# A Mamba-style scan with a gated low-rank feed-forward on one core: the layer-norm statistics of z from VectorE to ScalarE, and batches 1 and 2 given the division of work of batch 3

## The chip, the cores and the metric

One core of a Trainium2 chip runs the whole kernel. The metric is the device time in microseconds (us) of one execution. Three runs of the kernel before gave 533.24, 533.96 and 534.74 us, so the median is 533.96 us.

## What is computed

The inputs are x (4 batches, 512 rows, 512 channels), a context of 4 x 512 x 256, and weights. In the reference, cut to the part around the change:

```python
# hidden = ctx, z = layernorm(x)
u = silu(causal_conv4(in_proj_w @ hidden) + conv_b)
delta = softplus(dt_proj_w @ dt_lo + dt_proj_b)
state = state * exp(delta * A) + (delta * u) * B_t      # 16 states for each channel
y_t = sum over n of state[n] * C_t[n]
x = x + tanh(g_xattn) * (y + D * u) * silu(layernorm(x))
x = x + tanh(g_ffn) * ffn(layernorm(x))                 # router, top 2 of 32 groups, low rank
```

`layernorm` takes mean and variance over the last axis, with eps 1e-5. The x that stands as z is indexed so that a row of x is a channel of the scan: one 128 x 512 tile of x holds the 128 channels of one block, and its row statistics are what z of that block needs.

## The kernel before, in words

The work goes through 20 phases (`PHASE`, L46), f = 0 to 19. In batches 0 to 2 a phase is one block of 128 channels over all 512 steps: phases 0 to 3 are batch 0, 4 to 7 batch 1, 8 to 11 batch 2. Batch 3 is cut in two halves of 256 steps and takes phases 12 to 19. Below, a phase of the first three batches is called a block (block 4 is phase 4, the first of batch 1).

Within a block all engines go through 16 states, n = 0 to 15, in 8 pairs (pair p is n = 2p and 2p+1). For each state:

- ScalarE (ACT) makes the decay exp(delta * A) (`decay`, L1003, its activation L1016).
- The product dt*u*B is made in one of two ways. For the pairs in `POOL_SETS` (L24) GpSimd (POOL) multiplies du by B, broadcast over the partitions, two states in one 128x1024 instruction (`times_b`, L559, instruction L571), into one of two buffers `dbu`; the decay then goes into a PSUM bank. For the other pairs TensorE (PE) multiplies the transposed du by diagonal matrices of B (`make_dbu`, L747, L759) into a PSUM bank, and the decay goes to one of three SBUF tiles `da`. The diagonal matrices of a batch are made once: by POOL (`diagonals`, L531, L544), and for the batch's last PE pair by ACT (L986).
- VectorE (DVE) runs the scan (`scan`, L1240, L1267).
- The state is multiplied by C: by POOL in pairs (`times_c`, L574, L586), or by DVE one state at a time for the pairs in `PAIRS_BY_DVE` (L98 to L100; `times_c`, L1274, L1285). In the latter case the scan writes to PSUM and the bank is free only after the multiplication.
- PE adds the 16 products, transposed, into `p_y` (`add_y`, L774, L781).

There are three PSUM banks for these tiles (`BANKS`, `wait_for_bank`, L374), twelve state slots (`RING`), and three `da` tiles, so ACT can run only about three states ahead of DVE. Every engine has its order written out by hand in a loop over f and n: POOL L609 to L670, PE L849 to L906, ACT L1132 to L1189, DVE L1399 to L1457. All waits are on counting semaphores; an engine that waits holds all that stands behind it.

Beside the scan, block f carries: the convolution of block f+5 (`conv_first` on ACT at n = 12, L1182, then three taps on DVE at n = 10, 11, 12, L1436 to L1445; the tap at n = 10 waits for `conv_first`, L1214), softplus of block f+1, du of block f+1 on POOL (`times_u`, L549), z = silu of the normalised x (`silu_z`, L1027, with two table loads), the gate and residual of block f-1 (`gate_y` on DVE at n = 8 and 9, L1428 to L1430), and from block 5 and 6 on the feed-forward of rows finished earlier. In the turning blocks 3, 7 and 11 B and C of the next batch are stored and broadcast by SyncE (SP) (L491 to L510), and the new diagonals are made.

The statistics of z of block f+4 are taken in block f by DVE, with `bn_stats` and `bn_aggr` (`z_statistics`, L1229), at n = 1, or at n = 14 when block f is the first of a batch (L1411). Four small POOL instructions turn them into scale and bias for a whole batch (`scale_of_z`, L588), in the turning block after the C of pair 5 (L661). The x of batch b+1 that they read is loaded by SP in the first block of batch b, for b = 1 and 2 (L504 to L507):

```python
if k == 0 and b and b + 1 < B:
    eng.wait_ge(ve_x2, 2 * Q * b)
    for j in range(Q):
        load_x(b + 1, j)
```

that is in blocks 4 and 8, after `gate_y` of the block before has read the old x; in block 8 the store of row tile 2 stands ahead of it on SP (L498). The x of batches 0 and 1 is loaded in the prologue.

## Time and profile before

| | |
|---|---|
| median of three runs | 533.96 us |
| the profiled execution's own time | 533.53 us |
| its span, first to last instruction | 531.8 us |
| mean granted TensorE clock | 0.978 |
| TensorE matmul busy | 491.4 us (92%) |
| TensorE weight load busy | 368.0 us (69%) |
| VectorE busy | 462.9 us (87%) |
| ScalarE busy | 380.1 us (71%) |
| GpSimd busy | 451.9 us (85%) |

1.7 us of the own time lie around the span. The shares are means over the whole kernel; the prologue (to about 27 us) and the tail (from about 507 us) have other limits than the blocks between them. In the rows further down a window from one mark to the next is used: a mark is the moment at which DVE starts delta of the next block (L1226), at n = 7 of the present one. Marks stand at 39.16 (block 0), 66.06, 90.03, 119.06 (block 3), 146.12 (block 4), 174.64, 203.36, 234.04 (block 7), 262.77 (block 8), 292.58, 320.12, 351.49 (block 11) and 375.20 us (phase 12). A window busy to 98% on an engine has that engine as a bound; when several engines have it, a change on one of them gives nothing alone.

### The profile page before, as it was taken

The page shows a single profiled execution, that of the slowest core. Times are in us where ns is not written, and L with a number is a line of the kernel's source. Part 1 is how long each engine was busy: PE and PEld are TensorE (multiplying, and loading weights), DVE is VectorE, ACT ScalarE, POOL GpSimd, SP SyncE. Part 2 cuts the span into 40 slices and gives each one's busy share as a digit, 9 for nine tenths or more (in the row PEclk, how much of TensorE's full clock was granted, in tenths as well). Part 3 has the DMA queues.
Part 4 walks back from the last instruction along what each step waited for, and adds up shares of the span by engine and source line. Part 5 has one row for each costly group of instructions (what it writes and reads, how often), then busy time and mean ns, then how long its engine had stood idle before and what let it go on. Part 6 is the DMA issues. An engine that isn't in the chain of part 4 may idle for free.

```text
span 531.8 us, 9178 instructions
## 1 busy us (share of the span) xinstructions
PE 491.4 (92%) x3018; PEld 368.0 (69%) x3018; DVE 462.9 (87%) x846; ACT 380.1 (71%) x699; POOL 451.9 (85%) x327
## 2 busy tenths in 40 slices
PE   9989899998787999999999999999899999899688
PEld 5568788687676676668676777767566766676654
DVE  3799799799799999799999999798988989999852
ACT  4698848775876777866958776957868869768542
POOL 1389999959999999989999999889799898888910
PEclk9969799999999999999999999999999999999899
DMA  5595000126520001065230000077100000000001
GB/s 127 176 375 217 0 2 1 41 85 213 182 80 1 1 1 60 1 229 202 71 101 2 20 1 22 8 281 227 45 21 1 22 20 17 6 21 21 2 20 39
DMA packets 18704, 39.36 MB, mean 74 GB/s; under 512 B 5585, under 2 KB 6353, under 8 KB 18658
## 3 DMA queue, kind: packets, MB, share of 16 engines
q1 hardware_dynamic: 18658, 38.79, 21.4%
q8 instruction: 24, 0.39, 0.3%
q14 instruction: 22, 0.18, 0.1%
HBM read 34.33 MB, written 4.46 MB: 73 GB/s over the span
## 4 chain that ended last, share of the span: by engine, by line
PE 48%; POOL 19%; DVE 13%; ACT 10%; issue 9%; DMA 1%; DVEq 0%; SPq 0%; POOLq 0%; ACTq 0%
PE p_s L759 12%; PE p_y L781 11%; POOL state L586 9%; POOL dbu L571 7%; DVE state L1267 6%; PE p_v L814 5%; PE p_f L805 5%; PE p_tr L728 3%; PE p_v L691 2%; ACT da L1016 2%; DVE x L1216 2%; PE p_pr L703 2%; ACT pair_b L1000 1%; PE p_f L794 1%; PE p_pr L682 1%
## 5 line engine op out<-in xcount | busy, mean ns | idle before, releaser
L586 POOL TENSOR_TENSOR state<-state,c_bc 128x1024 f32<-128x1024 f32 (+1 forms) x131 | 256.7, 1970 | 21.6 <-DVE state L1267 19.2
L759 PEld LDWEIGHTS p_s<-pair_b,du_t 128*128 128x128 f32 x1072 | 140.7, 200 | 44.9 <-issue 33.4
L759 PE MATMUL p_s<-pair_b,du_t 128*128 128x128 f32 x1072 | 154.6, 287 | 16.0 <-DVE state L1267 15.8
L781 PE MATMUL p_y<-ident,state 128*128 128x128 f32 x1024 | 149.3, 276 | 0.0
L1016 ACT ACTIVATE p_s<-delta,a_neg 128x512 f32<-128x512 f32 (+1 forms) x162 | 93.7, 583 | 77.6 <-DVE state L1267 44.1
L1267 DVE TENSOR_TENSOR_SCAN state<-da,p_s 128x512 f32<-128x512 f32 (+1 forms) x116 | 134.5, 1172 | 16.0 <-PE p_s L759 13.1
L571 POOL TENSOR_TENSOR dbu<-du,pair_b 128x1024 f32<-128x1024 f32 (+1 forms) x80 | 145.3, 1819 | 0.2 <-DMA pair_b<-bc_rows 0.2
L781 PEld LDWEIGHTS p_y<-ident,state 128*128 128x128 f32 x1024 | 121.5, 144 | 23.3 <-issue 20.2
L1016 ACT ACTIVATE da<-delta,a_neg 128x512 f32<-128x512 f32 (+1 forms) x158 | 99.3, 647 | 18.5 <-DVE state L1267 18.4
L1267 DVE TENSOR_TENSOR_SCAN state<-p_s,dbu 128x512 f32<-128x512 f32 (+1 forms) x100 | 97.6, 996 | 7.6 <-POOL dbu L571 6.0
L805 PE MATMUL p_f<-u_sb,h_t 128*128 128x512 f32 x112 | 55.4, 597 | 2.4 <-DVE gw L1364 2.4
L814 PE MATMUL p_v<-v_sb,hug_t 128*128 128x512 f32 x112 | 55.4, 598 | 0.0
L1285 DVE TENSOR_TENSOR state<-p_s,c_bc 128x256 f32<-128x256 f32 (+1 forms) x58 | 30.5, 526 | 0.7
L544 POOL TENSOR_SCALAR_AFFINE_SELECT pair_b<-b_t 128x1024 f32<-128x1024 f32 x11 | 12.4, 1133 | 19.9 <-ACT b_t L972 19.9
L1267 DVE TENSOR_TENSOR_SCAN state<-p_s,carry,dbu 128x256 f32<-128x256 f32 x40 | 28.0, 734 | 0.8 <-POOL dbu L571 0.7
L805 PEld LDWEIGHTS p_f<-u_sb,h_t 128*128 128x128 f32 x112 | 18.5, 191 | 12.7 <-issue 9.6
L1267 DVE TENSOR_TENSOR_SCAN p_s<-p_s,dbu 128x512 f32<-128x512 f32 x22 | 26.8, 1217 | 0.0
L1216 DVE SCALAR_TENSOR_TENSOR u<-p_pr,cw,u 128x511 f32<-128x511 f32 (+2 forms) x33 | 24.1, 730 | 2.2 <-ACT u L936 2.1
L770 PEld LDWEIGHTS p_y<-ident,skipped 128*128 128x128 f32 x64 | 7.2, 143 | 24.5 <-issue 24.5
L814 PEld LDWEIGHTS p_v<-v_sb,hug_t 128*128 128x128 f32 x112 | 18.1, 190 | 8.4 <-issue 8.3
L556 POOL TENSOR_TENSOR du<-delta,u 128x512 f32<-128x512 f32 (+1 forms) x19 | 19.8, 1043 | 2.8 <-POOL dbu L571 2.8
L682 PE MATMUL p_pr<-cx,w_in 128*128 128x512 f32 x44 | 21.5, 612 | 0.0
(175 smaller groups left out, 640.6 us busy)
## 6 DMA issues: line engine op xcount, KB each, us to landing
c_bc<-bc_rows SPq DMA_DIRECT2D x32, 512.0 KB, 5.1
pair_b<-bc_rows SPq DMA_DIRECT2D x16, 512.0 KB, 5.5
xs<-in_x SPq DMA_DIRECT2D x16, 256.0 KB, 4.6
out<-ot SPq DMA_DIRECT2D x14, 256.0 KB, 2.0
cx<-in_ctx_t SPq DMA_DIRECT2D x4, 512.0 KB, 3.8
u_sb<-in_u_w SPq DMA_DIRECT2D x1, 1024.0 KB, 14.1
v_sb<-in_v_w SPq DMA_DIRECT2D x1, 1024.0 KB, 15.6
w_in<-in_in_w_t SPq DMA_DIRECT2D x1, 384.0 KB, 4.7
```

Source lines behind the costliest of these rows:

```text
L556: eng.tensor_tensor(du[:, 0:w], delta[:, f % 2, 0:w], u[:, (Q * b + k) % U_RING, c0:c0 + w], ALU.mult).then_inc(po_du, 1)
L571: eng.tensor_tensor(dbu[:, i % 2, :, 0:w], du[:, 0:w].unsqueeze(1).to_broadcast([P, 2, w]), rows_of_b(p)[:, :, c0:c0 + w], ALU.mult).then_ ...
L586: eng.tensor_tensor(pair, pair, c_bc[:, 2 * p:2 * p + 2, c0:c0 + w], ALU.mult).then_inc(po_cs, 1)
L682: mm = eng.matmul(conv_bank(q)[:, :], w_in[:, k, e * P:(e + 1) * P], cx[:, k, :], start=(k == 0), stop=(k == KD - 1))
L759: mm = eng.matmul(p_s[g % BANKS][:, t * P:(t + 1) * P], du_t[:, f % 2, t, :], diagonals_of(n // 2)[:, n % 2, c0 // P + t, :], start=(t == ...
L781: mm = eng.matmul(p_y[:, t, :], slot(NS * f + n)[:, t * P:(t + 1) * P], ident[:, :], is_transpose=True, start=False, stop=(n == NS - 1 and ...
L805: mm = eng.matmul(hu_bank(T)[:, :], ht_of(T)[:, k, :], u_sb[:, k, :], start=(k == 0), stop=(k == Q - 1))
L814: mm = eng.matmul(v_bank(T)[:, :], hugt_of(T)[:, k, :], v_sb[:, k, :], start=False, stop=(k == Q - 1), skip_group_check=True)
L1016: eng.activation(to, delta[:, f % 2, 0:w], ACT.Exp, scale=a_neg[:, k, n:n + 1]).then_inc(ac_da, 1)
L1216: eng.scalar_tensor_tensor(out=conv_v(q)[:, s:], in0=conv_bank(q)[:, 0:L - s], scalar=cw[:, q % Q, TAPS - 1 - s:TAPS - s], in1=conv_v(q)[: ...
L1267: eng.tensor_tensor_scan(scanned, decayed, added, first, ALU.mult, ALU.add).then_inc(ve_scan, 1)
L1285: eng.tensor_tensor(slot(g)[:, 0:w], scanned, c_bc[:, n, c0:c0 + w], ALU.mult).then_inc(ve_cs, 1)
```

## The change

Three things. (1) `z_statistics` of batches 1 to 3 goes from DVE to ACT, in three parts at n = 11, 12 and 13 of block f for block f+4, in every block f from 0 to 11: a copy with a summed output, a 128x1 activation that makes the negative mean, and a square of x minus mean with a summed output. DVE keeps only the four of batch 0. `scale_of_z` of batches 1 to 3 has three POOL instructions in place of four and moves from the turning block to the next block, between the C of pair 0 and of pair 1. (2) `POOL_SETS` of batches 1 and 2 goes from pairs 1, 3, 5, 7 to pairs 0, 2, 3, 5, 6, that of batch 3. (3) The C that DVE multiplies: before, pair 1 in blocks 3 to 11 and pair 5 in blocks 3, 7 and 11; after, pair 1 in blocks 1 and 2, and pairs 1 and 4 in blocks 4 to 11. Phases 12 to 19 are as before.

```diff
--- before.py
+++ after.py
@@ -21,7 +21,7 @@
 
 
 
-POOL_SETS = [[2, 5], [1, 3, 5, 7], [1, 3, 5, 7], [0, 2, 3, 5, 6]]
+POOL_SETS = [[2, 5]] + 3 * [[0, 2, 3, 5, 6]]
 
 
 def flamingo(nc, x, ctx_t, g_xattn, g_ffn, in_w_t, conv_w, conv_b, x_w_t, dt_w_t, dt_b, a_log, d_skip,
@@ -96,8 +96,8 @@
 
 
     PAIRS_BY_DVE = [(LAST, 7)]
-    PAIRS_BY_DVE += [(f, p) for f in range(SPLIT, F) for p in (1, 4)]
-    PAIRS_BY_DVE += [(f, 1) for f in range(Q - 1, SPLIT)] + [(f, 5) for f in range(Q - 1, SPLIT, Q)]
+    PAIRS_BY_DVE += [(f, p) for f in range(Q, F) for p in (1, 4)]
+    PAIRS_BY_DVE += [(f, 1) for f in (1, 2)]
     C_BY_DVE = [(f, n) for f in range(F) for n in range(NS) if (f, n // 2) in PAIRS_BY_DVE]
     C_BY_POOL = [(f, p) for f in range(F) for p in range(PAIRS) if (f, p) not in PAIRS_BY_DVE]
     c_by_dve = {tile: i for i, tile in enumerate(C_BY_DVE)}
@@ -202,6 +202,7 @@
         zst = sb("zst", [P, 6])
         zmv = sb("zmv", [P, Q, 2])
         zv = sb("zv", [P, 2, Q])
+        z_of = sb("z_of", [P, 3, Q])
         zr = sb("zr", [P, 2, 2, Q])
         zh = sb("zh", [P, 2, L])
         sz_t = sb("sz_t", [P, Q, P])
@@ -275,6 +276,7 @@
         ac_skip = sem("act_d_u")
         ac_pre = sem("act_residual_placed")
         ac_h = sem("act_h")
+        ac_zs = sem("act_z_statistics")
         ac_e = sem("act_exp_scores")
         ac_out = sem("act_out")
 
@@ -367,7 +369,11 @@
         def broadcasts_of_b(b, p):
             return sum(p in pool_pairs(a) for a in range(b + 1)) + (p == 0)
 
-        ZOPS = 4
+        def zops(b):
+
+
+            return 4 + 3 * b
+
         FOPS = 3
         GOPS = 9
 
@@ -586,15 +592,23 @@
                 eng.tensor_tensor(pair, pair, c_bc[:, 2 * p:2 * p + 2, c0:c0 + w], ALU.mult).then_inc(po_cs, 1)
 
             def scale_of_z(b):
-                eng.wait_ge(ve_zs, 2 * Q * (b + 1))
-                if b >= 2:
-                    eng.wait_ge(ac_z, Q * (b - 1))
+                if b:
+                    eng.wait_ge(ac_zs, 3 * Q * b)
+                    if b >= 2:
+                        eng.wait_ge(ac_z, Q * (b - 1))
+                    eng.tensor_scalar(zv[:, 0, :], z_of[:, 2, :], 1.0 / E, EPS, ALU.mult, ALU.add).then_inc(po_zs, 1)
+                    eng.wait_ge(po_zs, zops(b - 1) + 1)
+                    eng.tensor_tensor(zr[:, b % 2, 0, :], zv[:, 0, :], minus_half[:, :], ALU.pow).then_inc(po_zs, 1)
+                    eng.wait_ge(po_zs, zops(b - 1) + 2)
+                    eng.tensor_tensor(zr[:, b % 2, 1, :], z_of[:, 1, :], zr[:, b % 2, 0, :], ALU.mult).then_inc(po_zs, 1)
+                    return
+                eng.wait_ge(ve_zs, 2 * Q)
                 eng.tensor_tensor(zv[:, 0, :], zmv[:, :, 1], eps_c[:, :], ALU.add).then_inc(po_zs, 1)
-                eng.wait_ge(po_zs, ZOPS * b + 1)
+                eng.wait_ge(po_zs, 1)
                 eng.tensor_tensor(zr[:, b % 2, 0, :], zv[:, 0, :], minus_half[:, :], ALU.pow).then_inc(po_zs, 1)
-                eng.wait_ge(po_zs, ZOPS * b + 2)
+                eng.wait_ge(po_zs, 2)
                 eng.tensor_tensor(zv[:, 1, :], zmv[:, :, 0], zr[:, b % 2, 0, :], ALU.mult).then_inc(po_zs, 1)
-                eng.wait_ge(po_zs, ZOPS * b + 3)
+                eng.wait_ge(po_zs, 3)
                 eng.tensor_tensor(zr[:, b % 2, 1, :], zv[:, 1, :], minus_one[:, :], ALU.mult).then_inc(po_zs, 1)
 
             def scale_of_f(T):
@@ -629,6 +643,8 @@
                         diagonals(b, i)
                 for T in STATS.get(f - 1, [])[1:]:
                     scale_of_f(T)
+                if k == 0 and b and c0 == 0:
+                    scale_of_z(b)
                 times_c(f, 1)
                 if many and not five:
                     times_b(f, pairs[2])
@@ -658,7 +674,6 @@
                 if k and STATS.get(f):
                     scale_of_f(STATS[f][0])
                 if turning:
-                    scale_of_z(b + 1)
                     diagonals(b + 1, 1)
                 times_c(f, 6)
                 if next_first and len(pool_pairs(PHASE[f + 1][0])) == 5:
@@ -1024,9 +1039,28 @@
                 eng.activation(skipped[:, 0:w], u[:, (Q * b + k) % U_RING, c0:c0 + w], ACT.Copy,
                                scale=dsk[:, k:k + 1]).then_inc(ac_skip, 1)
 
+            def z_statistics(q, part):
+
+
+                b, k = q // Q, q % Q
+                if part == 0:
+                    eng.wait_ge(s_x[b % 2][k], 16 * (b // 2 + 1))
+                    eng.wait_ge(ve_dl, q - Q + 2)
+                    if b > 1:
+                        eng.wait_ge(po_zs, zops(b - 1))
+                    eng.activation(vsp[:, :], xs[:, b % 2, k, :], ACT.Copy,
+                                   accum_out=z_of[:, 0, k:k + 1]).then_inc(ac_zs, 1)
+                elif part == 1:
+                    eng.wait_ge(ac_zs, 3 * (q - Q) + 1)
+                    eng.activation(z_of[:, 1, k:k + 1], z_of[:, 0, k:k + 1], ACT.Copy, scale=-1.0 / E).then_inc(ac_zs, 1)
+                else:
+                    eng.wait_ge(ac_zs, 3 * (q - Q) + 2)
+                    eng.activation(vsp[:, :], xs[:, b % 2, k, :], ACT.Square, bias=z_of[:, 1, k:k + 1],
+                                   accum_out=z_of[:, 2, k:k + 1]).then_inc(ac_zs, 1)
+
             def silu_z(f):
                 b, k, c0, w = PHASE[f]
-                eng.wait_ge(po_zs, ZOPS * (b + 1))
+                eng.wait_ge(po_zs, zops(b))
                 eng.wait_ge(s_x[b % 2][k], 16 * (b // 2 + 1))
                 if f >= 2:
                     eng.wait_ge(pe_turn, TURN["sz", zh_before(f)] + 1)
@@ -1180,6 +1214,8 @@
                             copy_b(b + 1)
                     if n == 12 and f + 5 < BLOCKS:
                         conv_first(f + 5)
+                    if n in (11, 12, 13) and f + Q < BLOCKS:
+                        z_statistics(f + Q, n - 11)
                     if n == 15 and f < LAST:
                         copy_du(f + 1)
                     if f in SILU_Z and n == (0 if f == 1 or turning else 9):
@@ -1227,15 +1263,12 @@
                                          op0=ALU.max, op1=ALU.add).then_inc(ve_dl, 1)
 
             def z_statistics(q):
-                b, k = q // Q, q % Q
-                eng.wait_ge(s_x[b % 2][k], 16 * (b // 2 + 1))
+                eng.wait_ge(s_x[0][q], 16)
                 if q:
                     eng.wait_ge(ve_zs, 2 * q)
-                eng.bn_stats(zst[:, :], xs[:, b % 2, k, :]).then_inc(ve_zs, 1)
+                eng.bn_stats(zst[:, :], xs[:, 0, q, :]).then_inc(ve_zs, 1)
                 eng.wait_ge(ve_zs, 2 * q + 1)
-                if b:
-                    eng.wait_ge(po_zs, ZOPS * b)
-                eng.bn_aggr(zmv[:, k, :], zst[:, :]).then_inc(ve_zs, 1)
+                eng.bn_aggr(zmv[:, q, :], zst[:, :]).then_inc(ve_zs, 1)
 
             def scan(f, n):
                 b, k, c0, w = PHASE[f]
@@ -1408,8 +1441,6 @@
                     if f == 0 and n == 7:
                         eng.wait_ge(ve_k, 3)
                         eng.reciprocal(aw[:, :], p_y_rows[:, 2 * S:3 * S]).then_inc(ve_k, 1)
-                    if n == (1 if f % Q else 14) and f + Q < BLOCKS:
-                        z_statistics(f + Q)
                     if n == 2 and mid >= 0:
                         best_two(mid, 0)
                         best_two(mid, 1)
```

## Rows read from the trace of the kernel before

**Rows 1.** The page: busy time, share of the span and instructions of each engine

```profile
PE 491.4 (92%) x3018; PEld 368.0 (69%) x3018; DVE 462.9 (87%) x846; ACT 380.1 (71%) x699; POOL 451.9 (85%) x327
```

**Rows 2.** Windows from mark to mark: PE, PEld, DVE, ACT, POOL busy, clock

```profile
146.12:174.64 28.52, 22.60 (x159) 18.58 (x158) 28.11 (x50) 19.77 (x32) 28.16 (x17) 0.96 0.12 38
...
203.36:234.04 30.68, 30.68 (x183) 20.98 (x182) 27.22 (x46) 23.30 (x37) 29.22 (x15) 1.00 0.24 84
234.04:262.77 28.73, 28.16 (x188) 22.05 (x187) 26.97 (x43) 20.51 (x40) 28.16 (x18) 1.00 0.45 170
262.77:292.58 29.81, 27.96 (x180) 21.21 (x179) 28.86 (x51) 21.77 (x35) 29.44 (x17) 1.00 0.15 46
...
320.12:351.49 31.37, 31.37 (x189) 21.85 (x188) 27.33 (x47) 24.15 (x39) 28.15 (x15) 1.00 0.21 66
```

**Rows 3.** The chain that ended last, in order of time: start, us, what

```profile
43.45 0.67 ACT u L936
...
50.67 0.60 DVE zst L1234
...
116.72 2.36 POOL state L586
...
130.89 1.03 POOL zr L594
...
191.07 6.96 POOL state L586 x3
...
202.37 1.98 PE p_f L805 x4
204.35 0.89 PE p_s L759 x8
```

**Rows 4.** Groups by form: instructions, shapes, count, busy us, mean ns, idle before

```profile
L571 POOL TENSOR_TENSOR dbu<-du,pair_b 128x1024 f32<-128x1024 f32 x40 | 94.4, 2366 | 0.2 <-DMA pair_b<-bc_rows 0.2
L1285 DVE TENSOR_TENSOR state<-p_s,c_bc 128x512 f32<-128x512 f32 x24 | 16.4, 684 | 0.4
L544 POOL TENSOR_SCALAR_AFFINE_SELECT pair_b<-b_t 128x1024 f32<-128x1024 f32 x11 | 12.4, 1133 | 19.9 <-ACT b_t L972 19.9
L1033 ACT ACTIVATE zh<-xs,zr 128x512 f32<-128x512 f32 x12 | 9.7, 813 | 0.1
L963 ACT ACTIVATE vsp<-vsp 128x512 f32<-128x512 f32 x12 | 7.5, 621 | 0.0
L1088 ACT ACTIVATION_READ_ACCUMULATOR p_f<-p_f,nmx 128x1 f32 x14 | 2.7, 191 | 0.0
L1038 ACT ACT_TABLE_LOAD x15 | 19.2, 1283 | 0.3
```

**Rows 5.** Timeline of block 4, n = 9 to 11: DVE, SP and ACT

```profile
149.54 0.67 DVE L1301 TENSOR_TENSOR x<-p_y,xs 128x512 f32<-128x512 f32 x1
...
150.23 1.77 SPq L410 DMA_DIRECT2D xs<-in_x  x4
...
150.67 0.76 ACT L936 ACTIVATE u<-p_pr,cb,cw 128x512 f32<-128x512 f32 x1
...
151.84 0.73 DVE L1216 SCALAR_TENSOR_TENSOR u<-p_pr,cw,u 128x511 f32<-128x511 f32 x1
...
152.57 1.19 DVE L1267 TENSOR_TENSOR_SCAN state<-p_s,dbu 128x512 f32<-128x512 f32 x1
```

**Rows 6.** The loads of x issued at 150.23 and at 267.82, to landing

```profile
DMA to landing us min/median/max: 4.9/4.9/4.9
...
DMA to landing us min/median/max: 4.1/4.1/4.1
```

**Rows 7.** Timeline of blocks 4 and 8: POOL's C of pair 5, SP's load, DVE's tap

```profile
157.69 2.36 POOL L586 TENSOR_TENSOR state<-state,c_bc 128x1024 f32<-128x1024 f32 x1
...
267.82 3.41 SPq L410 DMA_DIRECT2D xs<-in_x  x4
...
269.34 0.75 DVE L1216 SCALAR_TENSOR_TENSOR u<-p_pr,cw,u 128x511 f32<-128x511 f32 x1 [0.44 <-ACT u L936]
```

## The prediction

> **What bounds the kernel now.** The page's shares come first [rows 1]: PE 92%, DVE 87%, POOL 85%, ACT 71%. Three engines are close together, so a mean says little; the windows from mark to mark say more [rows 2]. In block 4 to 5 (146.12 to 174.64) DVE is busy 28.11 and POOL 28.16 of 28.52 us, PE only 22.60. The windows up to 320.12 that are not at a turn of PE's load (from the marks of blocks 5, 7, 8 and 9) look alike: POOL at 98 to 99%, DVE at 94 to 99%. Only the two windows before and into a turn, 203.36 to 234.04 and 320.12 to 351.49, have PE at 100% and POOL with 1.5 and 3.2 us to spare. Last, the chain in order of time [rows 3] names the owner of each stretch: ACT in block 0 up to 46 us (its `conv_first` stands on it), then DVE with the statistics of z on it, PE to 116, POOL alone from 116.72 to 200 (rows of C products, 2.32 us apiece: 6.96 for three), and PE from 202 on, with ACT and DVE between its stretches in block 8. The reader is to see that time can be won only where all engines of a window have room.
>
> **The price of each part.** POOL's pair instruction is 2.36 us, 2.32 apart [rows 3, 4]. A C product on DVE is 0.68, some 0.6 of it as a step in the queue [rows 4]. A PE tile of `make_dbu` is 0.89 [rows 3]. The statistics on DVE are 0.60 on the chain [rows 3] and about 0.1 more for the aggregation: 0.7. A POOL diagonal is 1.1 [rows 4].
>
> On ACT the trace has no copy or square with a summed output. The copy lies between 0.62 (immediate operands) and 0.81 (two pointers), the square likewise with one pointer; each is followed by a read of the accumulator, 0.19 [rows 4]. The 128x1 step costs at least about 0.1 in the queue and at most the 0.19 of that read. I take 0.75 + 0.15 + 0.85 = 1.75 us a block (bounds 1.4 and 2.2). ACT has 7 to 9 us idle in each of the windows shown [rows 2], so its busy time alone moves nothing there. What counts is where it stands in the queue: the first pass is at n = 11, ahead of `conv_first` at n = 12, for which DVE's first tap at n = 10 waits.
>
> Work of an ordinary block of batches 1 and 2 (4, 5, 6, 8, 9, 10): POOL 5 products with B and 6 with C against 4 and 7, so nothing. DVE two C more (1.2), statistics less (0.7): +0.5. PE two tiles fewer: -1.8. In turning blocks 7 and 11 POOL has one more pair instruction (+2.3), and DVE the same C and no statistics: -0.7. Block 3: C of pairs 1 and 5 goes back to POOL. Blocks 1 and 2: pair 1 goes to DVE, POOL -2.3 and DVE +0.5 each, with PE on the chain: nothing. Over the kernel POOL has 8 products with B more and 6 with C fewer, two diagonals fewer (-2.2, at turns 3 and 7), and three short `scale_of_z` of three instructions, whose long one stays (1.03 [rows 3]): -0.3 each. SP issues two broadcasts of B more; all B it needs early is issued early, and PE's diagonals no longer use the pairs that POOL took, so I cost it at nothing; the cover is the six or more states before those pairs are scanned.
>
> **The sum, mark by mark, as a lag against before.**
> (a) Blocks 0 to 2. ACT's first pass stands on the chain in block 0 ahead of `conv_first` [rows 3]: +0.75. Two statistics leave DVE's part of the chain: -1.4. Lag -0.7.
> (b) Block 3. DVE saves two C and one statistics at n = 1 to 3 (1.9), so POOL's C of pair 2 comes at about 115.0 instead of 116.72. From there to the product of pair 3 in block 4, at which DVE waits today, POOL has today ten pair instructions, du, three diagonals and the scale of z (27.1 us, ending at 143.8); after, eleven, du and two diagonals (28.8, ending at 143.8). So nothing is won: lag -0.7 at mark 4.
> (c) The new wait in block 4. The x that the first pass reads at n = 11 is the x of batch 2. Its load goes out at 150.23, right behind `gate_y` (149.54 + 0.67), and lands after 4.9 [rows 5, 6]. Today nobody needs it before n = 14. After the change ACT, which is at n = 12 at 150.67, stands until it lands; `conv_first` stands behind it, and DVE's tap behind that. With C of n = 8 putting `gate_y` back by 0.6: landing 155.7, first pass 0.75, decay 0.62, `conv_first` 0.7, so the tap can start at 157.8. Without the wait it would start at 151.84 + 1.2 = 153.1. DVE stands 4.7 us. The scan of n = 11, which ends at 153.8 today, ends at 159.6. POOL today starts C of pair 5 at 157.69 [rows 7], 3.9 us after that scan; this distance absorbs part. From its own work POOL could start at 156.7, and stands 2.9 us. DVE has 0.4 idle in that window [rows 2] and regains nothing; POOL is full through blocks 4 to 6. By the scan of n = 6 in block 6, POOL's count gives +4.2 and DVE's +4.5 (it regains the 1.5 us that it waits there for POOL today); less the 0.7 of (a), the lag is +3.7.
> (d) Window 203 to 234. PE sets it at 30.68; after, 28.9, with POOL 29.2 of work but able to start earlier. -1.8: lag +1.9.
> (e) Window 234 to 262. PE 1.8 less, POOL +1.0 (a pair more, a diagonal less), ACT in a solid row: I take -0.9, lag +1.0.
> (f) The new wait in block 8. The load goes out at 267.82, behind the store, and lands after 4.1 [rows 6, 7]. The same addition: 0.4 later, landing 272.3, tap possible at 274.5 against 270.1 with the extra C (today 269.34, with 0.44 of waiting for ACT in it). Scan n = 11 is 0.8 + 4.3 later. POOL had run early, so the whole counts: lag +6.1.
> (g) Blocks 9 and 10 to 320: DVE and POOL full, small idle parts against +0.5 of C: lag +5.7. Window 320 to 351, PE-bound: -1.8, then a little into the turn, -0.4. Lag +3.5. Batch 3 and the tail are as before and keep it.
> 533.53 + 3.5 = 537.0 us. The profiled execution is 0.4 below the median of the runs, so against that it is +3.0. About 0.3% (1.6 us) is what a measurement of this kernel can tell from no change.
>
> **A rule weighed.** In the rows PE holds the chain in two long stretches and is 100% busy in two windows, though its weight loads are busy 21 to 22 of some 31 us there [rows 2]. The Trainium skill, page "Perfetto Trace Analysis", section "Identifying the Most-Contended Engine", says that matmul busy time is no good measure of TensorE's distance from its limit, and that weight-load busy time is a better one. By that, TensorE with 69% is the least loaded of the four and taking work from it gives nothing.
>
> **Rivals.**
> Rival 1, faster: the waits are absorbed. Place: blocks 4 and 8, between the tap at n = 10 and C of pair 5. Price: 4.7 and 4.3 us on DVE. For it: POOL is 3.9 us behind in block 4, and PE has 6 us idle in that window [rows 2, 7]. Against it: DVE is full, and in block 8 the tap already waits for ACT. It decides where x lands before ACT asks or the lag regained exceeds 6 us. Without both waits my steps leave -0.7, then -1.8, -0.4 and -1.9 partly limited by POOL: -3.0, 530.5 us. Chance 0.13.
> Rival 2, no difference: half of the waits is absorbed, 533.5 + 0.3 = 533.8 us. Chance 0.15.
> Rival 3, slower still: PE with less work gives nothing, because POOL and DVE have the same windows; (d), and the first part of the last step of (g), drop out: 537.0 + 1.8 + 1.8 = 540.6 us. For it: POOL 29.2 of 30.7 in the window of (d). Against it: 3.2 us of room before block 11. It decides when POOL's count reaches the pair products later than PE would. This is also where the page's rule of the last paragraph leads. Chance 0.20.
> Rival 4: ACT must load another table for each square. From the rows a load is 1.28, two for each of 12 blocks 31 us, of which ACT's idle time would hide half: about 550 us. In this kernel copy and absolute value run between exponentials with no load among them: the 15 loads of L1038 are those of the 15 silu groups [rows 4]. Chance 0.02. The Trainium skill, page "ScalarE: Activation LUTs", section "Table sets: the hidden batching unit", has cheap functions in every set, naming relu, copy, identity and abs; square is not in that sentence, and no row here shows it.
> My forecast: 0.50.
>
> **The numbers.** The likeliest case gives 537.0; its own range is 535 to 539, from the bounds of ACT's parts and of the landing. The 8 in 10 reach to 541 for rival 3, and down to 533 with most of rival 2. Rival 1, a small part of rival 2 and rival 4 are left out. Faster by over 0.3% is rival 1, 0.13; within it rival 2, 0.15; slower the forecast, rival 3 and rival 4, 0.72.
>
> **What would show it.** In the changed kernel DVE's taps should wait for ACT's `conv_first` for 4 to 5 us in blocks 4 and 8, and ACT for the load of xs just before; elsewhere the tap should wait under 1 us. Windows of blocks 4 and 8 should be 4 to 6 us longer, those of blocks 6 and 10 about 1.8 shorter with PE no longer at 100%. In batch 0 no window should differ by over 1 us. ACT's table loads at L1038's place should stay at 15. I am wrong if ACT does not stand before the landing, or if POOL is still at 98% in blocks 5 to 7 after the wait and the mark of block 7 has no lag.

## The result, and the profile after

The changed kernel takes 543.2 us (median of four runs, 542.46 to 543.5) against 533.6 us for the kernel before in the same job (532.96 to 534.74). The ratio is 1.0175, 95% interval 1.0154 to 1.0197. It is slower by 9.6 us between the medians (9.3 by the ratio), where the prediction had 3.0 against the median, 3.5 against the profiled execution, and a range to 541. The profiled execution took 543.2 us, its span 541.4. Times and ratios below are of runs at the usual granted clock; only product_later has others (580.92 and 597.97 us, at a mean clock of 0.932 and 0.822), and its trace is of the first of these.

The engines' totals on the page after, which answer to [rows 1]:

```profile
PE 485.9 (90%) x2890; PEld 357.7 (66%) x2890; DVE 460.9 (85%) x834; ACT 398.2 (74%) x759; POOL 454.4 (84%) x324
## 4 chain that ended last, share of the span: by engine, by line
PE 35%; POOL 28%; DVE 14%; issue 11%; ACT 8%; DMA 2%; DVEq 0%; SPq 0%; POOLq 0%; ACTq 0%
```

PE lost 5.5 us of work, DVE 2.0, POOL gained 2.5 and ACT 18, and every share but ACT's fell. On the chain that ended last PE fell from 48% to 35% and POOL rose from 19% to 28%. Work that merely moved cannot explain a longer time in which three engines are less busy; waiting can.

The windows between the same marks as before show where the time came in (after: 67.04, 120.07 and so on; same columns as [rows 2]):

```profile
38.87:67.04 28.17, 23.98 (x167) 21.45 (x168) 22.16 (x23) 23.24 (x43) 23.46 (x11) 0.88 0.30 111
...
120.07:148.41 28.34, 21.99 (x156) 18.86 (x154) 23.43 (x25) 20.49 (x40) 28.09 (x17) 0.94 0.61 215
148.41:181.54 33.13, 24.01 (x137) 18.72 (x136) 27.89 (x49) 21.58 (x38) 29.84 (x17) 0.81 0.11 33
181.54:212.29 30.75, 28.34 (x165) 20.94 (x164) 27.59 (x47) 22.66 (x39) 28.46 (x16) 0.93 0.00 1
212.29:242.03 29.74, 29.36 (x170) 19.56 (x169) 27.69 (x46) 24.91 (x42) 28.02 (x15) 1.00 0.21 75
...
271.40:303.00 31.60, 26.67 (x164) 19.36 (x163) 28.48 (x49) 22.66 (x40) 29.14 (x17) 1.00 0.14 43
303.00:332.10 29.10, 26.17 (x164) 19.37 (x163) 27.51 (x46) 23.66 (x41) 28.49 (x16) 1.00 0.03 10
```

Against the marks of before, the lag is +1.0 at mark 1, +2.3 at mark 4, +6.9 at 5, +8.9 at 6, +8.0 at 7, +8.6 at 8, +10.4 at 9, +12.0 at 10, +10.4 at 11 and +9.1 at 13, and stays there. The windows of blocks 4 and 8 hold the forecast waits (33.13 against 28.52, 31.60 against 29.81). But the windows from marks 5 and 9 hold no load of x and are 2.0 and 1.6 us longer all the same. In the last row above DVE has 1.6 us idle, POOL 0.6, PE 2.9. In the window before and into turn 7, PE's relief is there: 29.74 instead of 30.68, and PE, busy 29.36 us of it, is still the fullest engine.

Block 4 after, in the timeline, around the wait:

```profile
153.02 0.68 DVE L1318 TENSOR_TENSOR state<-p_s,c_bc 128x512 f32<-128x512 f32 x1
...
157.30 0.63 ACT L1051 ACTIVATE vsp<-xs 128x512 f32<-128x512 f32 x1 [5.19 <-DMA xs<-in_x]
158.54 0.76 ACT L951 ACTIVATE u<-p_pr,cb,cw 128x512 f32<-128x512 f32 x1
...
159.33 0.75 DVE L1252 SCALAR_TENSOR_TENSOR u<-p_pr,cw,u 128x511 f32<-128x511 f32 x1 [3.92 <-ACT u L951]
```

ACT stands 5.19 us for x; `conv_first` is behind it; the tap stands 3.92. In block 8 the same two waits are 3.3 and 2.4. The step that was forecast happened, somewhat smaller on DVE (3.9 and 2.4 for 4.7 and 4.3).

What was not forecast as a wait is in the sums of waits between 120 and 370 us (who <- for whom: us in all, times, longest):

```profile
DVE state L1300 <- POOL dbu L577: 10.2, 7, 4.3
ACT vsp L1051 <- DMA xs<-in_x: 8.4, 2, 5.2
DVE u L1252 <- ACT u L951: 6.6, 3, 3.9
POOL state L592 <- DVE state L1300: 5.9, 7, 2.0
```

DVE waits for POOL seven times, nearly always at n = 6, and POOL waits for DVE seven times. In the kernel before, between 120 and 360 us, DVE waited for the same tile twice:

```profile
DVE state L1267 <- POOL dbu L571: 4.1, 2, 2.7
```

Two engines that wait for each other in turn make a loop. One turn of it, POOL in block 5 and 6 and the scan that waits:

```profile
192.11 2.37 POOL L592 TENSOR_TENSOR state<-state,c_bc 128x1024 f32<-128x1024 f32 x1 [2.02 <-DVE state L1300]
194.44 2.37 POOL L577 TENSOR_TENSOR dbu<-du,pair_b 128x1024 f32<-128x1024 f32 x1
...
206.91 2.37 POOL L577 TENSOR_TENSOR dbu<-du,pair_b 128x1024 f32<-128x1024 f32 x1
209.31 1.22 DVE L1300 TENSOR_TENSOR_SCAN state<-p_s,dbu 128x512 f32<-128x512 f32 x1 [1.42 <-POOL dbu L577]
...
221.21 2.36 POOL L592 TENSOR_TENSOR state<-state,c_bc 128x1024 f32<-128x1024 f32 x1 [1.20 <-DVE state L1300]
```

From C of pair 5 (192.11, released by the scan of n = 11) POOL makes seven pair instructions and one `scale_of_f` until the product of pair 3 is there (209.3, 17.2 us); DVE goes from the scan of n = 6 to that of n = 11 with two C of pair 4 and its other work (11.9 us); then POOL starts C of pair 5 again (221.21). 29.1 us for a turn, and the window from mark 9 is 29.10. Before the change there was one pair instruction fewer in the first part and no C in the second; by the same rows that is about 25.6 us (an estimate: 29.1 less 2.3 and twice 0.6), shorter than any of these windows, so the loop did not bind.

The window from mark 5 is 30.75, though, and the loop is only 29.2 of it. The rest is a wait of DVE for PE at n = 9, between the scans of n = 6 and n = 11:

```profile
186.07 1.23 DVE L1300 TENSOR_TENSOR_SCAN p_s<-da,p_s 128x512 f32<-128x512 f32 x1 [1.56 <-PE p_s L774]
```

Three of the runs below have the same loop in this block and a shorter wait there: 0.63, 1.17 and 1.24 us with windows of 29.81, 30.35 and 30.41 (batch0_c2, behind_conv2, other_x). Window less wait is 29.2 each time. The wait falls behind a stretch of PE at the lower clock (see the last section). So in block 5 the loop made about 0.5 us of the 2.0, and in block 9, where the clock was at its full level throughout, all 1.6.

### The profile page after: what moved, and what is told of

Its sections match the earlier page's. It is cut to its first block, busy times and chain, and to the rows that moved or that the text cites. A ratio compares the mean times of both kernels' runs of the same rounds, so it can differ in the third digit from the quotient of the medians.

```text
span 541.4 us, 8962 instructions
## 1 busy us (share of the span) xinstructions
PE 485.9 (90%) x2890; PEld 357.7 (66%) x2890; DVE 460.9 (85%) x834; ACT 398.2 (74%) x759; POOL 454.4 (84%) x324
## 4 chain that ended last, share of the span: by engine, by line
PE 35%; POOL 28%; DVE 14%; issue 11%; ACT 8%; DMA 2%; DVEq 0%; SPq 0%; POOLq 0%; ACTq 0%
POOL state L592 15%; POOL dbu L577 11%; PE p_y L796 8%; PE p_s L774 8%; DVE state L1300 5%; PE p_v L829 4%; PE p_f L820 3%; DVE p_s L1300 3%; PE p_tr L743 3%; PE p_v L706 2%; ACT da L1031 2%; DVE x L1252 2%; ACT p_s L1031 1%; DMA xs<-in_x 1%; DVE x L1334 1%
## 5 line engine op out<-in xcount | busy, mean ns | idle before, releaser
L592 POOL TENSOR_TENSOR state<-state,c_bc 128x1024 f32<-128x1024 f32 (+1 forms) x125 | 243.4, 1955 | 26.2 <-DVE state L1300 24.0
L577 POOL TENSOR_TENSOR dbu<-du,pair_b 128x1024 f32<-128x1024 f32 (+1 forms) x88 | 164.8, 1872 | 0.2 <-DMA pair_b<-bc_rows 0.2
L774 PE MATMUL p_s<-pair_b,du_t 128*128 128x128 f32 x944 | 139.4, 290 | 25.4 <-DVE state L1300 17.3
L774 PEld LDWEIGHTS p_s<-pair_b,du_t 128*128 128x128 f32 x944 | 125.7, 202 | 49.6 <-issue 41.0
L1300 DVE TENSOR_TENSOR_SCAN state<-p_s,dbu 128x512 f32<-128x512 f32 (+1 forms) x138 | 143.4, 1055 | 17.6 <-POOL dbu L577 12.8
L1031 ACT ACTIVATE da<-delta,a_neg 128x512 f32<-128x512 f32 (+1 forms) x142 | 87.9, 640 | 12.8 <-DVE state L1300 12.7
L1300 DVE TENSOR_TENSOR_SCAN state<-da,p_s 128x512 f32<-128x512 f32 (+1 forms) x66 | 74.2, 1144 | 8.9 <-PE p_s L774 7.1
L1300 DVE TENSOR_TENSOR_SCAN p_s<-da,p_s 128x512 f32<-128x512 f32 (+1 forms) x52 | 54.8, 1054 | 3.4 <-PE p_s L774 3.2
L1318 DVE TENSOR_TENSOR state<-p_s,c_bc 128x512 f32<-128x512 f32 (+1 forms) x70 | 38.7, 553 | 0.7
L785 PEld LDWEIGHTS p_y<-ident,skipped 128*128 128x128 f32 x64 | 7.3, 147 | 27.1 <-issue 27.1
L987 ACT ACTIVATE sz_t<-p_tr,gx 128x512 f32<-128x512 f32 (+1 forms) x20 | 12.0, 602 | 14.9 <-PE p_tr L743 14.6
```

What stands on the lines that cost most here:

```text
L577: eng.tensor_tensor(dbu[:, i % 2, :, 0:w], du[:, 0:w].unsqueeze(1).to_broadcast([P, 2, w]), rows_of_b(p)[:, :, c0:c0 + w], ALU.mult).then_ ...
L592: eng.tensor_tensor(pair, pair, c_bc[:, 2 * p:2 * p + 2, c0:c0 + w], ALU.mult).then_inc(po_cs, 1)
L774: mm = eng.matmul(p_s[g % BANKS][:, t * P:(t + 1) * P], du_t[:, f % 2, t, :], diagonals_of(n // 2)[:, n % 2, c0 // P + t, :], start=(t == ...
L1031: eng.activation(to, delta[:, f % 2, 0:w], ACT.Exp, scale=a_neg[:, k, n:n + 1]).then_inc(ac_da, 1)
L1300: eng.tensor_tensor_scan(scanned, decayed, added, first, ALU.mult, ALU.add).then_inc(ve_scan, 1)
L1318: eng.tensor_tensor(slot(g)[:, 0:w], scanned, c_bc[:, n, c0:c0 + w], ALU.mult).then_inc(ve_cs, 1)
```

## The experiments

The three suspects are the wait for x, this loop, and batch 0. Twelve kernels were run. Ratios are to the kernel before in the same job.

**The two halves of the change.** Statistics alone: the changed file with the old division of work. The other half alone: the old file with the new one.

```diff
-POOL_SETS = [[2, 5]] + 3 * [[0, 2, 3, 5, 6]]
+POOL_SETS = [[2, 5], [1, 3, 5, 7], [1, 3, 5, 7], [0, 2, 3, 5, 6]]
```

(and the old `PAIRS_BY_DVE`; the other half is the reverse edit on the kernel before.)

> The statistics of z on ScalarE as in the change, with POOL_SETS and the division of the C products as before. Theory A (the waits for x in blocks 4 and 8 are most of the loss): ScalarE stands 3 to 5 us for the load in each of them, DVE's first tap stands behind it, and a good part reaches the end: 537 to 540 us. Theory B (a loop between GpSimd and VectorE in the five-pair order is most of the loss): the loop is not there, POOL is 3.9 us behind and absorbs the waits: 533 to 535.5 us.

Measured: 538.89 us, ratio 1.0094 (1.0062 to 1.0126).

> POOL_SETS and the division of the C products as in the change, the statistics of z on DVE as before. Theory A: no new wait for x, so about as before, 532.5 to 535 us. Theory B: the loop is there (pair 3's product stands seven pair instructions behind C of pair 5, and DVE has two more C products in it), the windows of blocks 5 and 9 stay 1.5 to 2 us longer than before and none of the batch 1 and 2 windows has an engine at 98%: 537 to 541 us.

Measured: 545.68 us, ratio 1.0204 (1.0167 to 1.0241), 4.7 us above what theory B allowed.

Neither half is free, and the new sets without the statistics are worse than the whole change. Theory A fails as the only cause (sets alone, with no wait for x at all, lose 11.5 us), and so does theory B: with the loop away the statistics still cost 4.7. In statistics alone mark 8 comes 1.0 us earlier than before, and then the window from mark 8 is 33.75 against 29.81 us. The waits there, between 262 and 297 us:

```profile
DVE u L1252 <- ACT u L951: 5.5, 1, 5.5
PEld p_s L774 <- ACT du_t L987: 5.4, 1, 5.4
PE p_s L774 <- DVE state L1300: 5.2, 1, 5.2
ACT vsp L1051 <- DMA xs<-in_x: 4.4, 1, 4.4
```

One wait of 5.5 us on DVE lengthened the window by 3.9; most of it was not absorbed, in a window in which DVE had 0.95 us and POOL 0.37 us idle before. In block 4 of the same run ACT stood 1.1 us for x and DVE 1.9 behind it, and that was absorbed: the window is 30.19 us, and 30.22 in stats_late below, which has no such wait.

**The wait for x taken away.** The changed kernel, reading other data at the two places:

```diff
+                here = (b - 1) % 2 if k == 0 and b > 1 else b % 2
                 if part == 0:
-                    eng.wait_ge(s_x[b % 2][k], 16 * (b // 2 + 1))
+                    if here == b % 2:
+                        eng.wait_ge(s_x[b % 2][k], 16 * (b // 2 + 1))
...
-                    eng.activation(vsp[:, :], xs[:, b % 2, k, :], ACT.Copy,
+                    eng.activation(vsp[:, :], xs[:, here, k, :], ACT.Copy,
```

> The changed kernel, but the statistics of the first block of batches 2 and 3 are taken from the x of the batch before (already loaded), so that ScalarE does the same work without waiting for a load; this part of z is scaled by the wrong statistics. Theory A: DVE's wait of 3.9 and 2.4 us at the tap goes and 5 to 7 us with it: 536 to 538 us. Theory B: the windows of blocks 4 and 8 get shorter by 2 us each at most, because the loop then sets their length too: 539 to 541.5 us.

Measured: 538.91 us, ratio 1.0094 (1.0061 to 1.0126). 4.3 us come back, between the two expectations. In the traces it is 3.0 in the window of block 4 (30.16 for 33.13) and 1.7 in that of block 8 (29.94 for 31.60), where DVE's waits had been 3.9 and 2.4: about a quarter of them had been absorbed. The loop remains:

```profile
DVE state L1302 <- POOL dbu L577: 10.5, 6, 4.3
POOL state L592 <- DVE state L1302: 6.1, 7, 1.7
```

**The same wait, with `conv_first` ahead of it.** The changed kernel:

```diff
-                    if n in (11, 12, 13) and f + Q < BLOCKS:
-                        z_statistics(f + Q, n - 11)
+                    if n in (12, 13, 14) and f + Q < BLOCKS:
+                        z_statistics(f + Q, n - 12)
```

> The changed kernel with ScalarE's statistics at n = 12, 13, 14, behind conv_first instead of ahead of it. ScalarE still stands for x in blocks 4 and 8. If the loss goes through DVE's tap that waits for conv_first: 3 to 4 us of the 4.3 come back, 539 to 540.5 us, and the tap waits under 1 us. If it goes through the decays behind the wait: 542 to 543.5 us.

Measured: 538.61 us, ratio 1.0093 (1.0062 to 1.0124), a little below the expected range. As much comes back as in other_x, but not all for the same reason: in the trace mark 1 already comes 0.65 us earlier than after the change, since in block 0, too, ACT's first pass now stands behind `conv_first`. The windows of blocks 4 and 8 give 2.9 and 1.7. The waits between 120 and 370 us:

```profile
ACT vsp L1051 <- DMA xs<-in_x: 0.9, 2, 0.6
DVE u L1252 <- ACT u L951: 0.3, 1, 0.3
```

One reserve: ACT itself stood only 0.9 us, since it asks later and since the load landed 2.3 us after its issue in block 4, not 4.1 to 4.4 as in the changed kernel. So this run fits the place ahead of `conv_first` as the fault, but some of it is a quicker load, and it does not separate the tap from the decays that also stood behind the wait.

**The loop shortened.** The changed kernel, in the blocks of batches 1 and 2:

```diff
+                early = five and w == L
+                if early:
+                    times_b(f, pairs[2])
                 times_c(f, 0)
-                if five:
+                if five and not early:
                     times_b(f, pairs[2])
-                elif many or len(pairs) == 3:
+                elif not early and many or len(pairs) == 3:
                     times_b(f, pairs[1])
```

> The changed kernel, but in the blocks of batches 1 and 2 POOL makes the product of pair 3 with B before C of pair 0 of the same block, one pair instruction (2.3 us) earlier in the loop. Theory A: the waits for x are untouched, 542.5 to 544 us. Theory B: the loop is shorter by up to 2.3 us a block in the blocks where it binds (5, 6, 8, 9, 10), DVE's wait for dbu at n = 6 (1.1 to 1.4 us in each) goes: 537 to 540.5 us.

Measured: 535.03 us (ten runs, 533.95 to 540.74), ratio 1.0032 (1.0002 to 1.0063). 8.2 us come back from exchanging two instructions whose work is the same, more than expected. Block 5's window and block 9's, the ones without any load, are now

```profile
177.31:205.69 28.38, 26.93 (x164) 19.76 (x163) 27.56 (x47) 22.28 (x39) 28.11 (x15) 0.95 0.00 1
295.33:322.94 27.61, 25.77 (x163) 19.25 (x162) 27.44 (x46) 22.73 (x40) 27.34 (x15) 1.00 0.03 10
```

instead of 30.75 and 29.10 us, with DVE or POOL at 99% again, and DVE's wait for dbu, in the same stretch, is 3.4 us in three places instead of 10.2 in seven. The windows to marks 4 and 5 gained 2.3 and 2.5, the second in part because ACT stood only 1.8 us for x there and not 5.2; those of blocks 5, 7 and 9 gained 2.4, 1.1 and 1.5. Of block 5's 2.4 us, 0.9 is DVE's shorter wait for PE at n = 9 (0.65 us).

**The loop lengthened**, by having the same product after C of pair 2:

```diff
-                if five:
+                if five and w < L:
                     times_b(f, pairs[2])
...
                 times_c(f, 2)
+                if five and w == L:
+                    times_b(f, pairs[2])
```

> The changed kernel with POOL's product of pair 3 one pair instruction later than in the change, after C of pair 2 instead of after C of pair 0 (C of pair 1 is DVE's), in the eight blocks of batches 1 and 2. The loop theory: 2.3 us for each of the blocks in which it binds, seven or eight: 557 to 562 us. If the gain of the earlier product came from something else (the scans' order against the banks): 543 to 548 us.

Measured: 570.69 and 575.58 us, ratio 1.073 (1.0687 to 1.0773); the median of all four runs is 578.25. The direction is right and the size above the expected range: 30 us more than the change, 3.7 a block. In the trace, whose own time is 580.92, DVE waits for POOL eight times, 34.6 us in all; the chain shows why it is two instructions' time and not one:

```profile
213.31 1.14 DVE state L1302
214.52 2.37 POOL state L592
216.89 2.31 POOL dbu L577
219.22 1.22 DVE state L1302
```

C of pair 2 must wait for the scan of n = 5, so the product comes two pair instructions (4.7 us) behind that scan, and the scan of n = 6 stands 4.2 us for it.

**The loop on the sets alone.** The same edit for the early product, on the kernel with the new sets and DVE's statistics.

> POOL_SETS and the C products as in the change, statistics on DVE, and POOL's product of pair 3 before C of pair 0. The loop theory: the same gain as on the changed kernel, 8 us, from 545.7 to 536 to 539 us; what is left above 534 is DVE's own work in the loop. If the gain on the changed kernel was from an interplay with ScalarE's statistics: 542 to 546 us.

Measured: 539.9 us, ratio 1.011 (1.0083 to 1.0136). 5.8 us come back, less than 8, and the time is 0.9 above the expected range. What remains above before, 5.6 us, is more than the changed kernel with the same edit has (535.03). In that kernel DVE has nothing of the statistics of batches 1 to 3: with two more C in a block on DVE, taking them off it is worth some 5 us, between runs of two jobs.

**Another place for DVE's C.**

```diff
-    PAIRS_BY_DVE += [(f, p) for f in range(Q, F) for p in (1, 4)]
+    PAIRS_BY_DVE += [(f, p) for f in range(SPLIT, F) for p in (1, 4)]
+    PAIRS_BY_DVE += [(f, p) for f in range(Q, SPLIT) for p in (1, 7)]
```

> The changed kernel with C of pair 7 instead of pair 4 by DVE in batches 1 and 2. Each engine has the same work; only the place changes. The loop theory: POOL has one pair instruction fewer between C of pair 5 and the product of pair 3 (2.3 us), and DVE 1.2 us less between the scans of n = 6 and n = 11, so it falls as with the earlier product: 534 to 539 us. If only the amount of work on each engine counts: 542.5 to 544 us.

Measured: 548.35 us, ratio 1.0254 (1.0228 to 1.028). Both expectations miss; it is slower than the change. The loop at n = 6 did go (two waits of DVE for dbu between 120 and 370 us instead of seven), but others came, here between 150 and 370 us:

```profile
POOL state L593 <- DVE state L1301: 14.0, 8, 3.3
ACT sz_t L988 <- PE p_tr L744: 13.4, 7, 3.2
...
PEld p_s L775 <- ACT h_t L988: 13.0, 5, 3.3
...
PE p_s L775 <- DVE state L1319: 11.9, 5, 3.1
```

With C of pairs 7 and 1 on DVE, at n = 14, 15, 2 and 3, PE waits for DVE to free banks just where it has the block's transposes and scores, and the chain from 180 to 247 us lies mostly on PE. I read it so; no run took that apart.

**Batch 0.** The changed kernel with batch 0's C as before the change:

```diff
-    PAIRS_BY_DVE += [(f, 1) for f in (1, 2)]
+    PAIRS_BY_DVE += [(Q - 1, 1), (Q - 1, 5)]
```

> The changed kernel, but in batch 0 DVE multiplies the same C as before the change (pairs 1 and 5 of block 3, none in blocks 1 and 2). If DVE's C of pair 1 in block 1 is what made the first window 1.3 us longer, and POOL's two more pair instructions in block 3 what made the window to mark 4 longer, mark 4 comes 3 to 5 us earlier and the time is 539 to 541 us. If the loop of batch 1 fills whatever is gained before it: 542.5 to 544 us.

Measured: 537.83 us, ratio 1.0071 (1.0043 to 1.0098). 5.4 us come back. Mark 4 was expected 3 to 5 us earlier and comes 3.7 earlier than in the changed kernel (1.4 earlier than before the change); the time is below the expected range. The window to mark 1 is 25.94 instead of 28.17, that to mark 4 26.51 instead of 28.34. Of the 2.2 us in the first, 1.5 are the two C products that stood on the chain there: from ACT's decays to PE's next `p_s` the chain takes 5.9 us after the change and 4.4 with this edit. The other 0.7 is that piece of PE itself, 2.05 us against 1.31 for the same eight matmuls, with more of it at the lower clock after the change. DVE in block 1 after the change and with this edit:

```profile
57.32 1.20 DVE L1300 TENSOR_TENSOR_SCAN p_s<-da,p_s 128x512 f32<-128x512 f32 x1
58.56 0.69 DVE L1318 TENSOR_TENSOR state<-p_s,c_bc 128x512 f32<-128x512 f32 x1
59.17 1.22 DVE L1300 TENSOR_TENSOR_SCAN p_s<-da,p_s 128x512 f32<-128x512 f32 x1
60.42 0.69 DVE L1318 TENSOR_TENSOR state<-p_s,c_bc 128x512 f32<-128x512 f32 x1
61.03 2.33 DVE L1300 TENSOR_TENSOR_SCAN state<-p_s,dbu 128x512 f32<-128x512 f32 x2
```

```profile
56.96 3.44 DVE L1300 TENSOR_TENSOR_SCAN state<-da,p_s 128x512 f32<-128x512 f32 x3 [2.96 <-PE p_s L774]
60.31 2.31 DVE L1300 TENSOR_TENSOR_SCAN state<-p_s,dbu 128x512 f32<-128x512 f32 x2
```

**Repairs put together.** The statistics of blocks 8 and 12 later, in blocks 4 and 8 only:

```diff
+                    if n in (11, 12, 13) and f + Q < BLOCKS and f not in (Q, 2 * Q):
+                        z_statistics(f + Q, n - 11)
+                    if n in (14, 15) and f in (Q, 2 * Q):
+                        z_statistics(f + Q, n - 14)
+                        if n == 15:
+                            z_statistics(f + Q, 2)
```

on the old division of work (stats_late), on the change with the early product (first_late), and on that with batch 0's C as before (first_late_batch0b).

> The kernel before with the statistics of z on ScalarE, those of blocks 8 and 12 at n = 14 and 15. The statistics at n = 11 to 13 gave 538.9, with the windows ahead of mark 8 1.0 us shorter in sum than before and the one from mark 8 3.9 us longer. If that 3.9 us is all from the wait for x: 532 to 534 us. If ScalarE's 1.75 us a block cost something of their own: 535 to 537 us.

Measured: 533.1 us, ratio 0.9976 (0.996 to 0.9992). The window from mark 8 is 28.18 us instead of 33.75: the loss of the statistics alone was the wait for x, and with it gone they are a small gain by themselves, together with the new place of `scale_of_z`.

> The changed kernel with two edits: POOL's product of pair 3 before C of pair 0 in batches 1 and 2, and ScalarE's statistics of blocks 8 and 12 (taken in blocks 4 and 8, for which x is still on its way) at n = 14 and 15 instead of 11 to 13. If the wait for x and the loop are two separate losses, both go: the product alone gave 535.0 and taking the wait away gave 4.3 us more on the changed kernel, so 530.5 to 532.5 us. If they are the same slack counted twice: 534 to 536 us.

Measured: 532.83 us, ratio 0.9979 (0.9967 to 0.999), 0.3 above the expected range: 2.2 us come back instead of 4.3. In the trace of product_first ACT's waits for x were 4.3 us in sum and not 8.4, so less was left to win. But 1.4 us of that is a load that landed sooner in block 4 (2.7 us after its issue, not 4.1), which no edit explains; how much the two losses truly share stays open.

> The changed kernel with the product of pair 3 before C of pair 0, the two late sets of statistics at n = 14 and 15, and batch 0's C as before the change. If the three losses add: 3 us below the 532.8 of the first two edits, 529.5 to 531.5 us, the fastest so far. If POOL in batch 1 takes back what batch 0 gains: 532 to 533.5 us.

Measured: 527.94 us (527.48 to 528.07), ratio 0.9892 (0.9874 to 0.991): the fastest and below the expected range, 6 us below the kernel before, 15.3 below the change. The single repairs sum to 8.2 + 4.3 + 5.4 = 17.9. The waits of this kind that remain between 120 and 370 us:

```profile
DVE state L1307 <- POOL dbu L577: 2.4, 3, 1.2
POOL du L562 <- POOL dbu L577: 1.4, 8, 0.2
DVE u L1259 <- ACT u L954: 0.3, 1, 0.3
```

So the change had a gain in it, and three losses laid over it: two of order (the place of the product, the place of the statistics in blocks 4 and 8) and the C that it moved in batch 0. How much of the 6 us is the better division of work is not shown, since no run gives the kernel before the early product as well; the statistics alone are about 1 us of it (stats_late).

## Why the prediction was wrong

The direction, and one of the mechanisms, were right; the size was about a third of what was measured (3.5 us against 9.7 on the profiled executions), and the range ended at 541. Two terms that were put at nothing failed: POOL's part in the price of an ordinary block, which left out the place of the product of pair 3 in POOL's row, and the C products that DVE takes in blocks 1 and 2.

The lag, forecast and measured, was -0.7 and +2.3 at mark 4, +3.7 and +8.9 at mark 6, +1.9 and +8.0 at mark 7, +1.0 and +8.6 at mark 8, +6.1 and +10.4 at mark 9, +5.7 and +12.0 at mark 10, +3.5 and +9.1 in batch 3. So 3.0 us of the miss stand at mark 4, 4.6 more come by mark 8 and 2.0 in block 9; block 8 gives 3.3 back.

- Step (a), blocks 0 to 2, lag -0.7: measured +1.2 at mark 2. ACT's first pass was the 0.7 us that was taken: put behind `conv_first` it makes mark 1 come 0.65 earlier (behind_conv2). "Blocks 1 and 2: pair 1 goes to DVE ... with PE on the chain: nothing" is the failed term: PE's `p_s` stands behind DVE's scans and C on the chain there, and two C put 1.5 us on it. Giving batch 0 its old C back was worth 5.4 us at the end. The gain from the statistics was larger than taken: with them on ACT and the work otherwise divided as before (stats_late), mark 2 comes 1.3 earlier and mark 4 3.0 earlier than before.
- Step (b), lag -0.7 at mark 4: measured +2.3. The count from C of pair 2 to the product of pair 3 was right (28.8 us; measured from 117.2 to 146.1), though the "ten pair instructions" of the kernel before are nine in its rows; its 27.1 us was read, not added up. The start of the count was not: taken at 115.0, it was 117.2, because block 3 itself came 1.0 us late and because POOL's C of pair 1, which the change puts back on POOL, stands directly ahead of it. The chain in order of time, in block 3 after the change, against 116.72 in [rows 3]:

```profile
113.61 1.23 DVE state L1300
114.91 4.68 POOL state L592 x2
119.59 2.32 POOL dbu L577
```

  I had let those 2.3 us fall into POOL's idle time. DVE then stood 4.34 us for the product at n = 6 of block 4, against 2.67 before. It is the same product that the loop turns on, and making it earlier gave 2.3 us in this window.
- Step (c), the wait in block 4: right. ACT 5.2 us, DVE 3.9 instead of 4.7. Step (f), block 8: right in kind, 2.4 instead of 4.3, in part by chance: the load took 2.6 us there and not the 4.1 that was taken. Block 8 grew by 1.8 us where 5.1 were forecast, which hid part of the other misses. Together the waits cost 4.3 us (other_x), and rival 1's question has the answer that about three quarters of them were not absorbed.
- Price of an ordinary block: "POOL ... nothing", "DVE ... +0.5". This is the largest step that failed. It added up work for each engine and then let the lag of POOL behind DVE be free. The order of POOL's row puts seven pair instructions between C of pair 5 and the product of pair 3 where six stood, and two C between the scans of n = 6 and n = 11: a loop of 29.1 us, over the 27.5 to 28.7 of blocks 5 and 9. Steps (c) and (g) assumed +0.5 a block at most and even that DVE regains 1.5 us before block 6; measured +2.0 in block 5 (of which 1.6 is the wait for PE at n = 9, also not forecast) and +1.6 in block 9. Step (e) took -0.9 in the window from mark 7, measured +0.6. The early product, which changes no engine's work, gave 8.2 us back, 2.3 of them already at mark 4 in its trace.
- Step (d), PE's relief: -0.9 in the window from mark 6 (taken 1.8); in (g), -1.6 in that from mark 10 (taken 1.8). PE's busy time fell by 1.3 and 2.0 us there and it stayed the fullest engine (29.36 of 29.74 and 29.37 of 29.75 us), so the windows followed it. With the early product they are 29.98 and 29.74 us, with PE and POOL both at 99% or more. Rival 3, that less work on PE gives nothing, is not borne out, and neither is what the prediction drew from the Trainium skill, page "Perfetto Trace Analysis", section "Identifying the Most-Contended Engine": its weight loads were busy 19.56 of 29.74 us in the window from mark 6, yet TensorE had no room there.
- ACT's parts: 0.62 and 0.71 for the passes, 0.19 for each read and for the small step, inside the bounds; 1.9 us a block in sum where 1.75 was taken, and 18 us more of busy time in all, since neighbours overlap. The small step on a 128x1 operand costs as much as the read. The table loads stayed 15 (rival 4 out), and the squares needed none.
- "What would show it": the waits for x and at the tap were there, PE left 100% in both windows (99%). The window of block 4 grew by 4.6 us as forecast, that of block 8 only by 1.8. "In batch 0 no window should differ by over 1 us" was false (1.27), and "elsewhere the tap should wait under 1 us" was false in blocks 0 and 2 (1.64 and 1.26, against 1.02 and 0.65 before).

Open: why the sets with DVE's statistics keep 5.6 us with the loop repaired was not taken apart, nor PE's waits with C of pair 7.

## What to carry to other kernels

When two engines hand work to each other and both are over 90% busy, adding up each one's work is not enough: follow the row of instructions from one hand-over round to the same hand-over in the next block, and count what stands between, on both engines. An instruction that is moved within its engine's row can be worth more than one that is moved to another engine. And before a read is moved to an engine that runs ahead of the others, look at when its data land, and at what stands behind it in that engine's row.

## What the runs showed of the hardware

The same first load of x (256 KB, issued by SP in block 4) landed 4.9 us after its issue in the kernel before [rows 6], 2.7 us in product_first and 2.3 us in behind_conv2; in the changed kernel the loads issued from 153.1 took 4.1 to 4.4, the first of block 8 2.6. A wait for a load had no fixed price even within one kernel.

The granted clock of TensorE has two levels in these traces, 1.00 and 0.50 (2.4 and 1.2 GHz). On the chain after the change eight matmuls of `p_s` take 1.72 us at 64.16, at the lower level, and 0.89 us at 74.54, at the full one. In the window of block 4 the mean was 0.81, against 0.96 before. Between 120 and 190 us the kernel before has one stretch at the lower level, 3.4 us from 144.8; the changed kernel has four, 20.4 us in all, from 141.6, 148.4, 162.0 and 179.1. In the window ahead of block 4's PE was busy 21.99 of 28.34 us, and 21.99 of 27.06 before. From 120 to 190 us the chain lay on POOL, DVE, ACT and the load of x, with no piece of PE, so most of these stretches cost nothing that can be seen; the last one goes with the 1.56 us that DVE waited for PE in block 5. No run sets the clock, so that is a reading.

The lower mean clock is not what made the change slow: the trace of product_first has 0.965, against 0.962 after the change and 0.978 before, and its time is 533.95 us. Among the ten runs of product_first the two slowest (540.74 and 537.86 us) do have the two lowest clocks (0.959 and 0.962). With the losses repaired the mean clock was 0.977.
